# Decoder of two layers on one core: rounding work of the feed-forward stage shared out anew, a shared residual addition, and another order of the first expert units

## The reference

```python
x = x + L0_attn(layernorm(x))          # 16 heads, causal, gated
x = x + L0_xattn(layernorm(x), ctx)
x = x + L0_ffn(layernorm(x))           # quantised, below
x = x + L1_attn(layernorm(x))          # 16 heads ("second" in the kernel)
x = x + L1_xattn(layernorm(x), ctx)    # one wide head ("wide")
x = x + L1_ffn(layernorm(x))           # experts, below
```

```python
# L0_ffn: bit-linear, depthwise convolution over tokens, silu, bit-linear
def act_quant(x):                       # per token
    scale = 127.0 / clip(max(abs(x), -1), 1e-5)
    return clip(round(x * scale), -128, 127) / scale
def weight_quant(w):
    scale = 1.0 / clip(mean(abs(w)), 1e-5)
    return clip(round(w * scale), -1, 1) / scale
h = act_quant(x) @ weight_quant(w1).T   # 256 -> 1024
h = silu(depthwise_conv1d(h, conv_w, conv_b))   # 3 taps
y = act_quant(h) @ weight_quant(w2).T   # 1024 -> 256

# L1_ffn: 16 experts, 2 chosen per token, and 2 shared ones
hidden = silu(x @ gate_e) * (x @ up_e)  # width 128 for each expert e
out = sum over e of combine[:, e] * (hidden_e @ down_e)
out = out + sh_hidden @ sh_down.T       # shared part, width 256 = 2 x 128
```

## Time and profile before

| what | value |
|---|---|
| median of 3 runs | 3332.97 us (3329.95 to 3334.74) |
| the profiled execution's own time | 3322.87 us |
| its span, from the first to the last instruction | 3321.6 us |
| busy: PE, PEld, DVE | 3142.9, 1709.7, 2293.2 us |
| busy: ACT, POOL | 1788.3, 631.7 us |
| granted TensorE clock, mean | 0.999 of full speed |

### The profile page before, as it was taken

How to read it: one execution, slowest core, us unless ns; L and a number is a source line. 1 busy time by engine, 2 the same in 40 slices (tenths; PEclk the granted TensorE clock), 3 DMA queues, 4 the chain that set the end, 5 groups by cost and what they waited for, 6 DMA issues and landing times. The chain is left out here.

```text
span 3321.6 us, 47034 instructions
## 1 busy us (share of the span) xinstructions
PE 3142.9 (95%) x17604; PEld 1709.7 (51%) x17604; DVE 2293.2 (69%) x4283; ACT 1788.3 (54%) x2567; POOL 631.7 (19%) x1182
## 2 busy tenths in 40 slices
PE   6999889999999989999999998999999999899999
PEld 4544433378645443337864544334786444433487
DVE  7855688566685578856678457884667845798455
ACT  3565556653456555664355555566434655656632
POOL 0322010024122201012412120101341311100033
PEclk9999999999999999999999999999999999999999
DMA  3322021023131202212312020220232212022023
GB/s 137 50 35 41 1 39 30 15 66 116 29 54 27 40 1 39 36 32 63 107 39 43 17 40 1 45 33 28 74 96 42 41 23 33 15 34 33 10 85 97
DMA packets 124680, 148.56 MB, mean 45 GB/s; under 512 B 31577, under 2 KB 82113, under 8 KB 124173
## 3 DMA queue, kind: packets, MB, share of 16 engines
q1 hardware_dynamic: 124452, 145.56, 20.3%
HBM read 75.04 MB, written 4.46 MB: 24 GB/s over the span
## 5 line engine op out<-in xcount | busy, mean ns | idle before, releaser
L800 DVE TENSOR_REDUCE small<-psum 128x1 f32<-128x512 f32 (+6 forms) x1856 | 1127.0, 656 | 208.8 <-PE psum L650 191.2
L760 ACT ACTIVATE work<-psum 128x1024 f32<-128x1024 f32 (+5 forms) x1024 | 917.5, 935 | 423.5 <-PE psum L678 322.4
L650 PE MATMUL psum<-work 96*128 96x512 bf16 (+4 forms) x2688 | 643.5, 307 | 32.6 <-DVE small L800 17.3
L1935 PE MATMUL psum<-rounded_work 128*128 128x512 f32 x2592 | 596.0, 391 | 9.9 <-DVE rounded_work L2021 6.5
L678 PE MATMUL psum<-work 99*128 99x512 bf16 (+4 forms) x2048 | 564.1, 358 | 15.6 <-ACT work L760 12.3
L1935 PEld LDWEIGHTS psum<-rounded_work 128*128 128x128 f32 x2592 | 485.8, 188 | 114.0 <-DVE rounded_work L2021 8.3
L712 PE MATMUL psum<-work 128*32 128x512 f32 (+4 forms) x4480 | 508.4, 526 | 1.6 <-ACT work L760 1.4
L650 PEld LDWEIGHTS psum<-work 96*128 96x128 bf16 x2688 | 234.3, 97 | 522.1 <-DVE small L800 329.1
L678 PEld LDWEIGHTS psum<-work 99*128 99x128 bf16 (+1 forms) x2048 | 177.3, 97 | 199.0 <-ACT work L760 67.8
L2036 ACT CAST rounded_work<-work 128x512 fp32r<-128x512 f32 x144 | 89.4, 621 | 342.9 <-DVE work L2077 321.4
L850 POOL CAST small<-small 128x16 bf16<-128x16 f32 x96 | 18.8, 196 | 938.0 <-issue 570.0
(11 more groups left out here) (288 smaller groups left out, 3750.8 us busy)
## 6 DMA issues: line engine op xcount, KB each, us to landing
work<-work SPq DMA_DIRECT2D x640, 96.0 KB, 3.0
work<-combine SPq DMA_DIRECT2D x64, 512.0 KB, 4.1
work<-in_w_gate SPq DMA_DIRECT2D x64, 128.0 KB, 3.5
work<-in_w_up SPq DMA_DIRECT2D x64, 128.0 KB, 3.4
work<-in_w_down SPq DMA_DIRECT2D x64, 128.0 KB, 3.8
work<-in_x SPq DMA_DIRECT2D x8, 512.0 KB, 4.8
out<-x SPq DMA_DIRECT2D x8, 512.0 KB, 2.9
work<-work SPq DMA_DIRECT2D x128, 14.4 KB, 1.9
```

The costliest lines, as they stand in the source:

```text
L650: ins = nc.tensor.matmul(dst[:, c * n:(c + 1) * n], A.q_pair[0:ROWS, slot, h, P * i:P * (i + 1)], A.k_of(pair, h)[0:ROWS, s0:s0 + n], star ...
L760: nc.scalar.activation(probs[0:size, n % PROBS, :, 0:P * many], banks(2 * (n % 2), 2)[0:size, :, 0:P * many], ACT.Exp, scale=DH ** -0.5).t ...
L800: nc.vector.tensor_reduce(tops[:, pair % 2, places[0]:places[-1] + 1:step], src, AX.X, ALU.max) \
L1935: ins = nc.tensor.matmul(dst, a_parts[i], b_parts[j], start=start and n == 0, stop=stop and n == 2, skip_group_check=True)
```

## The change

It has five parts. (a) In step 1 of the feed VectorE raises tiles 0 to 2 and ScalarE tiles 3 to 7. (b) In step 2 the running largest of slice 5 is taken after the loop's last convolution and not within the turn of slice 7. (c) In step 4 ScalarE rounds slices 0, 2, 4 and 6 and VectorE 1, 3, 5 and 7, VectorE scales in the order 0, 2, 1, 4, 3, 6, 5, 7, and TensorE's constant matmuls are 12 and three times 2 in place of 6 and 6. (d) In step 5 tiles 2, 3, 6 and 7 are scaled by ScalarE into `fed_scaled` and added to `x` by GpSimd; VectorE takes their statistics after that. (e) The first four expert units are (expert 0, half 0), (1, 0), (0, 1), (1, 1); before, they were (0, 0), (0, 1), (1, 0), (1, 1). The waits for weights and places follow the units.

```diff
--- before.py
+++ after.py
@@ -1482,7 +1482,7 @@
                 ins = nc.tensor.matmul(flat_banks(6, 2)[:, P * i:P * (i + 1)], widen(q_scale[:, i:i + 1], P), ident[:, :], start=True, stop=True)
                 if i % 4 == 3:
                     ins.then_inc(*up("rows_spread", i // 4))
-            busy_tensor(6, 0)
+            busy_tensor(12, 0)
             for mm in range(NH):
                 pe.wait_ge(*at(QUANTISED[by_scalar_rounded(mm)], mm))
                 for i in range(NT):
@@ -1490,8 +1490,8 @@
                                            start=(mm == 0 and i % 2 == 0), stop=(mm == NH - 1), skip_group_check=True)
                     if mm == NH - 1 and i % 2:
                         ins.then_inc(*up("fed", i // 2))
-                if mm == 0:
-                    busy_tensor(6, 0)
+                if mm in (1, 2, 4):
+                    busy_tensor(2, 0)
             busy_tensor(26)
             for j in range(NT // 2):
                 turn_tensor("feed", j)
@@ -1499,13 +1499,20 @@
                     second_unit_tensor(0)
                     busy_tensor(2)
 
-        QUANTISED = ("even_quantised", "odd_quantised")
+        QUANTISED = ("odd_quantised", "even_quantised")
+
+
+        SCALED = (0, 2, 1, 4, 3, 6, 5, 7)
+        RAISED_BY_VECTOR = 3
 
         def by_scalar_rounded(mm):
-            return mm % 2 == 1 and mm < NH - 1
+            return mm % 2 == 0
 
         def feed_scalar():
             nc.scalar.activation(small[:, 432:433], ident[:, 0:1], ACT.Silu)
+            act.wait_ge(*at("numbers_scaled"))
+            for i in range(RAISED_BY_VECTOR, NT):
+                nc.scalar.activation(xn[:, i, :], xn[:, i, :], ACT.Identity, bias=rounders[:, 0:1], scale=q_scale[:, i:i + 1]).then_inc(*up("rows_raised", i))
             for j in range(NT // 2):
                 turn_scalar("quantised", j)
             for mm in range(NH + 1):
@@ -1521,12 +1528,15 @@
                     if mm >= 4:
                         act.wait_ge(*at("raised", mm - 3))
                     nc.scalar.activation(absolute[:, (mm - 1) % 2] if mm > 1 else hi, conv[:, mm - 1, :], ACT.Abs).then_inc(*up("absolute", mm - 1))
-            for mm in range(1, NH - 1, 2):
+            for mm in range(0, NH, 2):
                 act.wait_ge(*at("hidden_scaled", mm))
                 nc.scalar.activation(conv[:, mm, :], conv[:, mm, :], ACT.Identity, bias=rounders[:, 0:1]).then_inc(*up("hidden_raised", mm))
                 act.wait_ge(*at("hidden_raised", mm))
                 nc.scalar.activation(hq[:, mm, :], conv[:, mm, :], ACT.Identity, bias=rounders[:, 1:2]).then_inc(*up(QUANTISED[1], mm))
             nc.scalar.activation(small[:, 432:433], ident[:, 0:1], ACT.Sqrt)
+            for n, i in enumerate(FED_BY_GPSIMD):
+                act.wait_ge(*at("fed", i // 2))
+                nc.scalar.activation(fed_scaled[:, n, :], fed(i), ACT.Identity, scale=q_inv[:, i:i + 1]).then_inc(*up("fed_scaled", i))
             root_scalar("feed", 0)
             norm_rows_scalar("feed")
             turn_scalar("feed", 0)
@@ -1536,16 +1546,27 @@
             turn_scalar("feed", 2)
             turn_scalar("feed", 3)
 
+
+        FED_BY_GPSIMD = (2, 3, 6, 7)
+        fed_scaled = absolute[:, 0, :].rearrange("p (i d) -> p i d", d=D)
+
+        def feed_gpsimd():
+            for n, i in enumerate(FED_BY_GPSIMD):
+                pool.wait_ge(*at("fed_scaled", i))
+                nc.gpsimd.tensor_tensor(x[:, i, :], x[:, i, :], fed_scaled[:, n, :], ALU.add).then_inc(*up("fed_added", i))
+
         def feed_vector():
             dve.wait_ge(*normed("cross", HT - 1))
             dve.wait_ge(*normed("cross", NT - 1))
             own(nc.vector.tensor_reduce(q_top, xn[:, :, :], AX.X, ALU.max, apply_absolute_value=True))
             own(nc.vector.tensor_scalar(q_top, q_top, 1e-5, None, ALU.max))
             quantiser(wscale[:, 0:1], "numbers_scaled")
-            for i in range(NT):
+            for i in range(RAISED_BY_VECTOR):
                 ins = nc.vector.tensor_scalar(xn[:, i, :], xn[:, i, :], q_scale[:, i:i + 1], ROUND, ALU.mult, ALU.add)
             own(ins)
             for i in range(NT):
+                if i >= RAISED_BY_VECTOR:
+                    dve.wait_ge(*at("rows_raised", i))
                 nc.vector.tensor_scalar(xn[:, i, :], xn[:, i, :], ROUND, q_inv[:, i:i + 1], ALU.subtract, ALU.mult).then_inc(*up("vector_norm", "normed", "quantised", i))
             w = resident["conv_w"]
             for mm in range(NH + 1):
@@ -1556,11 +1577,12 @@
                                                        op0=ALU.mult, op1=ALU.add))
                     nc.vector.scalar_tensor_tensor(out=c[:, 0:T - 1], in0=h[:, 1:T], scalar=w[:, mm, 2:3], in1=c[:, 0:T - 1],
                                                    op0=ALU.mult, op1=ALU.add).then_inc(*up("convolved", mm))
-                if mm >= 3:
-                    dve.wait_ge(*at("absolute", mm - 2))
-                    if mm > 3:
-                        dve.wait_ge(*at("raised", mm - 3))
-                    nc.vector.tensor_tensor(hi, hi, absolute[:, (mm - 2) % 2], ALU.max).then_inc(*up("raised", mm - 2))
+
+                for raising in (mm - 2,) if 3 <= mm < NH - 1 else (NH - 3, NH - 2) if mm == NH else ():
+                    dve.wait_ge(*at("absolute", raising))
+                    if raising > 1:
+                        dve.wait_ge(*at("raised", raising - 1))
+                    nc.vector.tensor_tensor(hi, hi, absolute[:, raising % 2], ALU.max).then_inc(*up("raised", raising))
             dve.wait_ge(*at("tops_turned", 0))
             own(nc.vector.tensor_reduce(q_top, flat_banks(4, 2).rearrange("p (i b) -> p i b", i=NT), AX.X, ALU.max, apply_absolute_value=True))
             dve.wait_ge(*at("tops_turned", 1))
@@ -1568,7 +1590,7 @@
             own(nc.vector.scalar_tensor_tensor(out=q_top, in0=q_last, scalar=1e-5, in1=q_top, op0=ALU.max, op1=ALU.max))
             quantiser(wscale[:, 1:2], "hidden_scale")
             dve.wait_ge(*at("rows_spread", 1))
-            for mm in range(NH):
+            for mm in SCALED:
                 ins = nc.vector.tensor_tensor(conv[:, mm, :], conv[:, mm, :], flat_banks(6, 2), ALU.mult)
                 if by_scalar_rounded(mm):
                     ins.then_inc(*up("hidden_scaled", mm))
@@ -1576,9 +1598,12 @@
                     own(ins)
                     nc.vector.tensor_scalar(hq[:, mm, :], conv[:, mm, :], ROUND, ROUND, ALU.add, ALU.subtract).then_inc(*up(QUANTISED[0], mm))
             for i in range(NT):
-                dve.wait_ge(*at("fed", i // 2))
-                own(nc.vector.scalar_tensor_tensor(out=x[:, i, :], in0=fed(i), scalar=q_inv[:, i:i + 1], in1=x[:, i, :],
-                                                   op0=ALU.mult, op1=ALU.add))
+                if i in FED_BY_GPSIMD:
+                    dve.wait_ge(*at("fed_added", i))
+                else:
+                    dve.wait_ge(*at("fed", i // 2))
+                    own(nc.vector.scalar_tensor_tensor(out=x[:, i, :], in0=fed(i), scalar=q_inv[:, i:i + 1], in1=x[:, i, :],
+                                                       op0=ALU.mult, op1=ALU.add))
                 norm_vector("feed", i)
 
 
@@ -1857,6 +1882,14 @@
         out_turned = work[:, OUT_AT:OUT_AT + KD * T].rearrange("p (h k t) -> p h k t", h=2, k=KD)
         out_row = lambda i: bank(4 + i // 2)[:, D * (i % 2):D * (i % 2 + 1)]
         NEXT_UNIT = 8
+
+        def expert_unit(u):
+
+            return ((0, 0), (1, 0), (0, 1), (1, 1))[u] if u < 4 else divmod(u, 2)
+
+        def last_unit(e):
+            return [u for u in range(2 * e, 2 * e + 3) if expert_unit(u) == (e, 1)][0]
+
         GATE_UP, DOWN = slice(0, 2 * D), slice(2 * D, 3 * D)
         SHARED = 2
         LAST = NE + SHARED - 1
@@ -1922,11 +1955,11 @@
                 if e >= SHARED:
                     pool.wait_ge(*at(EXPERT_LOADED[e % 2], e, 2))
                 if e >= 2:
-                    pool.wait_ge(*at("unit_projected", 2 * e - 3))
+                    pool.wait_ge(*at("unit_projected", last_unit(e - 2)))
                 cut(e, GATE_UP, gate_up).then_inc(*up("gate_cut", e))
                 pool.wait_ge(*at("gate_cut", e))
                 if e >= 2:
-                    pool.wait_ge(*at("unit_down", 2 * e - 3))
+                    pool.wait_ge(*at("unit_down", last_unit(e - 2)))
                 cut(e, DOWN, down).then_inc(*up("down_cut", e))
                 pool.wait_ge(*at("down_cut", e))
 
@@ -1944,7 +1977,7 @@
 
         def expert_tensor():
             def down(u):
-                e, half = divmod(u, 2)
+                e, half = expert_unit(u)
                 pe.wait_ge(*at("unit_ready", u))
                 pe.wait_ge(*at("down_cut", e))
                 if u == 0:
@@ -1983,9 +2016,9 @@
                     ins.then_inc(*up("weights_turned"))
                     down(u - 2)
                     pe.wait_ge(*at("combine_turned"))
-                if u < 2:
+                if u in (0, 2):
```

(3 more changed lines are left out.)

## The result

| | median us | runs | granted clock of the runs |
|---|---|---|---|
| kernel before, at the prediction | 3332.97 | 3 | |
| kernel before, with the runs beside the changed one | 3330.19 (3325.20 to 3334.74) | 6 | |
| changed kernel | 3306.55 (3303.95 to 3310.13) | 6 | 0.998 in five, 0.996 in one |

The ratio of the changed kernel to the one before is 0.9935, 95% interval 0.9921 to 0.9949: faster by 0.65%, 17 to 26 us. Forecast were 3314.3 us in a range of 3310 to 3322, 18.7 us less.

The account below looks back on a forecast made before the run. TensorE was taken to bound second attention (busy 224.17 of 232 us) and experts (102 of 102), VectorE the feed's rounding. 1.35 + 0 + 1.13 + 0.57 + 1.62 = 4.67 us a trip, 18.7 in four, gave 3314.3 us, range 3310 to 3322.

Parts of the forecast that it names:

- (a): First rounding in the feed: TensorE's first turn and the projection start earlier, 1.35 us a trip taken, 1.1 as lower end.
- (b): The running largest in the feed: the order on VectorE stays the same, so the gain is 0.
- (c): Second rounding in the feed: slice 7 starts 1.13 us earlier, waiting for its input and not its turn on TensorE.
- (d): Residual sum in the feed: GpSimd's adds at 742 ns bring the combining forward, 0.57 us a trip beyond (c)'s gain.
- (e): Expert units: TensorE's wait before unit 1 for the rows of half 1 goes, 1.62 us a trip passing whole.
- the base: Forecast's last step: the 18.7 us gain from the profiled execution is taken off the runs' median, giving 3314.3 us.
- the sentence on the second half: Feed's residual sum, within (d): rows of tiles 4 and 5 are ready before TensorE has done its projection.
- more than the sum: Rival, chance 0.08: VectorE and ScalarE run ahead in the second half, up to 0.4 us a trip more, 3311 to 3313.
- The sum: All five parts' gains added: 4.67 us a trip, 18.7 in four.
- The gain is not given back: Denies a rival, chance 0.08: attention plan or experts absorb the gain, 1.5 us a trip remain, 3327, no difference.
- TensorE's clock as a rival: Chance 0.04: pauses at 408 to 409 drop the clock to 1.2 GHz until the second attention; 5.7 us net loss, 3356.

## Why the prediction was right and wrong

In short: the parts (a), (b) and (c) came as worked out, (d) and (e) were right in mechanism and too small by 0.3 us each, and the step that carried the time out of its range is the base, "I take the same 18.7 off the median".

**(a)** 1.35 forecast, 1.30 measured. ScalarE's raises took 2.57 us, near the lower end of the 2.5 to 2.9 that was worked out, and its copies followed without a pause.

**(b)** 0, and 0 measured.

**(c)** 1.13 forecast, 1.13 measured, in the kernel with (c) alone as well. Slice 7 waits for its input and no longer for its turn, as the timeline of TensorE's weight loads shows:

```profile
419.18 0.77 PEld L1489 LDWEIGHTS psum<-w2q,work 128*128 128x128 bf16 x8 [0.21 <-DVE work L1599]
```

**(d)** 0.57 forecast, 0.63 measured up to the first projection; ScalarE's scaling took 474 ns and not the 586 of L474. The rule of the Trainium skill (GPSIMD Engine Reference, Engine selection) that elementwise adds are about twice as slow on GpSimd does not decide here: the add took 726 ns against VectorE's 468 for scale and add together, 1.55 times as long and not twice, and what counts is that it ran beside VectorE. The step of (d) that failed is the sentence on the second half, that VectorE's rows are ready before TensorE has done its projection. That holds for tiles 4 and 5. Tiles 6 and 7 came from VectorE only at 430.7 before, and TensorE's second pair of turns, begun at 430.12, waited inside a merged row: 1.30 for eight matmuls that take 1.04. In its timeline:

```profile
429.33 1.38 DVE L461 TENSOR_SCALAR xn<-x,small 128x256 f32<-128x256 f32 x4
```

Four tiles in 1.38 end at 430.71, 0.59 after the turns began. Worth 0.25 a trip. A gain in the second half was among the rivals ("more than the sum", chance 0.08), but put down to the early last slice, which is (c)'s: with (c) alone the distance stays at 4.27, with (d) alone it is 4.02.

**(e)** 1.62 forecast, 1.94 measured. The mechanism was right, the size was read from the wrong number. The row's 1.65 us are counted from the modelled end of the last matmul, 0.39 behind its start, while in an unbroken row of these matmuls the next one starts 0.23 behind (0.16 more); and behind the wait the second matmul follows the first by 0.33 and not 0.23 (0.10 more). From trip 1 of the changed kernel, 18 matmuls take 1521.15 - 1516.96 = 4.19; of the kernel before, TensorE's timeline has

```profile
700.46 1.62 PE L1935 MATMUL psum<-rounded_work 128*128 128x512 f32 x6
```

so that from the first of its six to the router were 706.58 - 700.46 = 6.12. The difference, 1.93, is the gain.

**The sum.** 1.30 + 1.13 + 0.63 + 0.25 + 1.94 = 5.25 a trip, 21.0 in four, against 18.7. The gain is not given back: from the second projection of the second attention to the first expert matmul, that is, second attention and wide together, it takes 265.6 to 266.2 us in all profiles, before and after.

**The base.** The larger share of the miss, 5.4 of 7.8 us, is the step "I take the same 18.7 off the median"; with 21.0 in place of 18.7 it would have given 3312.0, inside the range. The median lay 10.1 us above the profiled execution, and the prediction left that unexplained. What orders the runs is the granted clock. Over the 58 runs of the kernel before, the mean time is 3334.9 us at a reading of 0.995 (8 runs), 3332.1 at 0.996 (9), 3329.1 at 0.997 (11), 3325.8 at 0.998 (13), 3322.4 at 0.999 (12) and 3321.0 at 1.000 (5): some 3 us for each 0.001. The profiled execution (3322.87 at 0.999) fits these means. The three runs of the prediction (3329.95 to 3334.74) have no clock on record, so theirs is an inference: of the 58, only runs at 0.995 to 0.997 took that long. Three runs from the slow end were luck of the draw; the median of the 58 is 3327.0, and 18.7 off that is 3308.3, 1.8 above the measured time. The changed kernel's first six mostly read 0.998. At that reading the two kernels have 3325.8 and 3305.9 (5 runs), 19.9 us apart. Here luck had a part too: in six later runs the changed kernel itself had a mean clock of 0.9958 and 3310.90 us, inside the range.

**TensorE's clock as a rival.** It was forecast as a loss from pauses at the second weights, with the reading that every stretch shows 1.00. There it stayed at 1.00 in all profiles. But the earlier trace rows are three windows of trip 0, and the same trace has 0.50 in its trip 3 (3170 to 3172 us, shown above; expert stretch 22.0 in place of 20.4). The clock falls in the router's product without a pause, and in the own attention.

The best kernels here are the changed one with its router split (3302.47 us, 8.4 us below the changed kernel on the same chip) and its two variants with filling in the own attention, which can't be told from it.

## What to carry to other kernels

Before a gain is taken off a median, explain how the median stands to the profiled execution; here the granted clock of each run orders the runs, and kernels are compared at the same reading or by stretches at full clock. Measure a removed wait by start to start against the pitch of the matmuls, not by its idle row, and look for waits inside merged rows: count times pitch against the row's length. Where TensorE does several microseconds of narrow matmuls, look at the granted clock there, and try to break them up with wide ones that have to be done anyway, best in a place where it waits.

## What was not expected of the hardware

TensorE's granted clock fell to 0.50 with no idle time in the windows around it: in or just behind 3.64 us of matmuls of 16 columns, in 24 of 32 trips, at 1.6 or 3.2 us a time. The Trainium skill (TensorE: Matmul & The Clock Gate, Part 1: The HAM clock gate) says that the clock is set by how busy the PE has been recently. By the busy time that the profile counts, this trace doesn't agree, since the busy share in those windows is 100%; what else about the router's product brings the fall is not shown. Why one trip in four escapes in kernels that are otherwise alike stays open.
